# A fused embedding, interaction and MLP kernel on one core: the second contraction and the MLP of a chunk moved into one step, layer 0 a slice earlier, one transpose replaced by a DMA

## What is computed

```python
e = stack([tbl_f[ids[:, f]] for f in range(39)], axis=1)      # [1024, 39, 16]
X0 = e; Xi = X0; res = []
for W, b in ((W0, b0), (W1, b1), (W2, b2)):                    # 128 outputs each
    Wr = W.reshape(128, 39, Xi.shape[1])
    Xi = einsum('hjk,bjd,bkd->bhd', Wr, X0, Xi) + b[None, :, None]
    res.append(Xi.sum(axis=2))
h = concatenate(res + [dense_ctx], axis=1)                     # [1024, 400]
h = maximum(h @ W_top1 + b_top1, 0.0)                          # 512
h = maximum(h @ W_top2 + b_top2, 0.0)                          # 256
y = h @ W_top3                                                 # [1024, 1]
```

## Time and profile before

| | us |
|---|---|
| median of 3 runs | 1438.17 (1437.16 to 1438.38) |
| the profiled execution, its time | 1436.21 |
| its span, first to last instruction | 1434.4 |
| PE busy | 1313.6 (92%) |
| DVE busy | 1082.4 (75%) |
| ACT busy | 1066.5 (74%) |
| POOL busy | 892.8 (62%) |
| mean granted PE clock | 0.972 of 2.4 GHz |

### The profile page before, as it was taken

One profiled execution on the slowest core, in us unless ns is written; L12 is line 12 of the kernel. 1 busy time (PEld: TensorE's weight loads), 2 busy tenths in 40 slices (PEclk: granted clock), 3 DMA queues, 4 the chain that ended last, 5 costly groups with the idle time before them and its releaser, 6 DMA issues.

```text
span 1434.4 us, 23609 instructions
## 1 busy us (share of the span) xinstructions
PE 1313.6 (92%) x6157; PEld 1061.7 (74%) x6157; DVE 1082.4 (75%) x2678; ACT 1066.5 (74%) x3372; POOL 892.8 (62%) x663
## 2 busy tenths in 40 slices
PE   3179999999999999999999999999999999999986
PEld 3158777777788777887778777887778878887765
DVE  3068989898867987688766988679876988679930
ACT  2238888789867887688867888678876899678942
...
DMA packets 53451, 87.27 MB, mean 61 GB/s; under 512 B 15136, under 2 KB 37152, under 8 KB 52032
## 3 DMA queue, kind: packets, MB, share of 16 engines
...
q10 hardware_dynamic: 156, 0.48, 0.1%
...
## 4 chain that ended last, share of the span: by engine, by line
PE 54%; POOL 19%; issue 12%; DVE 8%; DMA 3%; ACT 2%; SPq 1%; ACTq 0%; POOLq 0%; DVEq 0%
PE ring L927 12%; PE ring L929 11%; PE ring L928 11%; POOL pairs L396 6%; POOL pairs_lo L407 6%; PE side L825 5%; POOL e_in L364 5%; PE l_ps L812 3%; DVE terms L754 3%; POOL blocks L418 3%; PE side L851 3%; PE l_ps L814 3%; PE l_ps L813 2%; DVE x_s L709 2%; DMA x_rep<-x_t 2%
## 5 line engine op out<-in xcount | busy, mean ns | idle before, releaser
L597 ACT ACTIVATE terms<-ring,e_both 128x128 f32<-128x128 f32 x2944 | 832.2, 399 | 242.9 <-PE ring L929 237.4
L754 DVE SCALAR_TENSOR_TENSOR terms<-ring,e_both,terms 128x128 f32<-128x128 f32 x1792 | 508.4, 344 | 96.7 <-PE ring L929 93.6
L927 PE MATMUL ring<-w_hi,x_hi 128*128 128x512 f32 (+1 forms) x1280 | 546.4, 427 | 32.5 <-DVE terms L754 25.2
L929 PE MATMUL ring<-w_hi,x_lo 128*128 128x512 f32 (+1 forms) x1280 | 500.4, 391 | 0.0
L928 PE MATMUL ring<-w_lo,x_hi 128*128 128x512 f32 (+1 forms) x1280 | 498.8, 390 | 0.0
L709 DVE TENSOR_REDUCE x_s<-terms 128x32 f32<-128x800 f32 x512 | 489.0, 976 | 0.2
L364 POOL DMA_INDIRECT e_in<-in_tbl,idx x312 | 305.8, 980 | 88.6 <-issue 79.0
L407 POOL TENSOR_TENSOR pairs_lo<-pairs,pairs_hi 117x1024 fp32r<-117x1024 f32 (+1 forms) x104 | 250.0, 2404 | 168.0 <-ACT pairs_hi L497 167.0
L927 PEld LDWEIGHTS ring<-w_hi,x_hi 128*128 128x128 f32 x1280 | 242.9, 190 | 106.8 <-DVE terms L754 38.5
L396 POOL TENSOR_TENSOR pairs<-x_rep,pairs 117x1024 f32<-117x1024 f32 (+1 forms) x104 | 250.4, 2408 | 93.2 <-DMA pairs<-x_t 93.2
L928 PEld LDWEIGHTS ring<-w_lo,x_hi 128*128 128x128 f32 x1280 | 243.6, 190 | 49.1
...
## 6 DMA issues: line engine op xcount, KB each, us to landing
pairs<-x_t SPq DMA_DIRECT2D x312, 156.0 KB
...
e_in<-in_tbl,idx POOLq DMA_INDIRECT x312
...
```

The lines of the kernel that those rows point to most:

```text
L597: last = nc.scalar.activation(term(d, ACT_BEFORE[d][g] + i), twos(ring[:, (GROUPS * d + g) % RING, i * H:(i + 1) * H]), ACT.Copy, scale=e_ ...
L754: nc.vector.scalar_tensor_tensor(out=acc, in0=y, scalar=e_of[:, j, d:d + 1], in1=acc, op0=ALU.mult, op1=ALU.add).then_inc(dve_unit, 1)
L927: nc.tensor.matmul(acc, x1_hi[:, x], w1_hi[:, w], start=True, stop=False)
L929: nc.tensor.matmul(acc, x1_lo[:, x], w1_hi[:, w], start=False, stop=True).then_inc(y_group, 1)
```

## The change

1. The table of places: layer 0's tiles 0 to 6 are made a slice earlier (7 to 13), tile 7 stays in slice 15; a tile is multiplied at groups 4 and 6; x1 of the first half leaves at (14, 7) and (14, 9), z0 at (15, 7).
2. x0t goes from slices 6, 7 to 5, 6, with the copies of the gathered rows (`COPY_SLICE`, `MOVE_SLICE`) a slice earlier, and the gathers are spread anew.
3. G of chunk c-1 is done in step c at groups 2, 5, 8 of slices 2, 3, 4, 7, 8 and at (9, 1); its blocks are made a slice ahead, with 4 slots in place of 3.
4. The MLP of chunk c-1 follows in the same step, slices 9 to 14. Step 9 is gone.
5. `xb` comes no longer from PE: `e_cur` is stored with d outermost, written to DRAM (`x0_write`, 128 x 16 x 39, after pair tile 11 on SP) and read back (`xb_back`, at the head of the next step).
6. G's columns are kept in groups: the evacuation (`evacuate_g`) reads and writes runs of 8, where before it wrote every 16th word; z0, dense and h2 are reordered to match; a block has its samples innermost.
7. `dense_t` has 128 rows, 112 of them zero, so that all of h1's matmuls have 128 rows.
8. SP's program is written out instead of looped.

```diff
-    Z2_SLICES, Z2_FROM, Z2_AT_ONCE = (0, 1, 2), 4, 2
-    XB_SLICES, XB_AT = (0, 1), 6
-    DENSE_SLICE = 2
-    H1_SLICE, H1_AT = 3, (6, 7, 8, 9)
-    H2_SLICE = 4
-    Y_SLICE, Y_AT = 5, 7
-    COPY_SLICE, CUR_FROM, MOVE_SLICE = 2, 4, 5
-    X0T_SLICES = (6, 7)
-    G_FIRST = 8
+    Z2_SLICES, Z2_FROM, Z2_AT_ONCE = (9, 10, 11), 4, 2
+    DENSE_SLICE = 11
+    H1_SLICE, H1_AT = 12, (6, 7, 8, 9)
+    H2_SLICE = 13
+    Y_SLICE, Y_AT = 14, 7
+    COPY_SLICE, CUR_FROM, MOVE_SLICE = 1, 3, 4
+    X0T_SLICES = (5, 6)
+    G_AT = [(d, g) for d in (2, 3, 4, 7, 8) for g in (2, 5, 8)] + [(9, 1)]
+    G_OUT_AT = [(d, g + 3) if g < 7 else (d + 1, 1) for d, g in G_AT]
...
-    L0_AT = [(1, 2) if d == D - 1 else (3, 5) for d in range(D)]
-
-    X1_HI_AT = {1: (6, 7), 0: (15, 4)}
-    X1_LO_AT = {1: (7, 1), 0: (15, 6)}
-    Z0_AT = {1: (7, 7), 0: (15, 8)}
+    L0_AT = (4, 6)
+
+    X1_HI_AT = {1: (6, 7), 0: (14, 7)}
+    X1_LO_AT = {1: (6, 9), 0: (14, 9)}
+    Z0_AT = {1: (7, 7), 0: (15, 7)}
...
-    BLOCK_FIRST, BLOCK_SLOTS = 7, 3
-
-    GATHERS = (3, 3, 3, 3, 3, 0, 6, 5, 1, 1, 2, 2, 1, 2, 1, 3)
-    INDEX_SLICE = 6
+    BLOCK_SLOTS = 4
+
+    GATHERS = (3, 2, 2, 2, 0, 5, 5, 1, 2, 2, 2, 2, 2, 2, 4, 3)
+    INDEX_SLICE = 5
...
+                def x0_write():
+
+                    after(sp, e_cur_ready, c + 1)
+                    after(sp, xb_in, 16 * c)
+                    sp.dma_start(x0_dram.rearrange("d b f -> b d f"), e_cur).then_inc(x0_out, 16)
+
+                def xb_back():
+
+                    after(sp, x0_out, 16 * c)
+                    after(sp, block_made, G_GROUPS * (c - 1))
+                    sp.dma_start(xb[:, :, :], x0_dram.rearrange("d (b g) f -> (d b) g f", g=G_GROUPS)
+                                 ).then_inc(xb_in, 16)
...
-                        nc.scalar.activation(e_cur[:, :, :], e_mid[:, 0:FIELDS, :], ACT.Copy).then_inc(e_cur_ready, 1)
+                        after(act, x0_out, 16 * c)
+                        nc.scalar.activation(e_cur, e_mid[:, 0:FIELDS, :].rearrange("p f d -> p d f"),
+                                             ACT.Copy).then_inc(e_cur_ready, 1)
...
                     nc.scalar.activation(
-                        g_t[:, :, g::G_GROUPS],
-                        side[:, g % 2, 0:SAMPLES_PER_G * GCOLS].rearrange("p (b j) -> p j b", j=GCOLS),
+                        g_t[:, :, g * SAMPLES_PER_G:(g + 1) * SAMPLES_PER_G],
+                        side[:, g % 2, 0:SAMPLES_PER_G * GCOLS].rearrange("p (j b) -> p j b", j=GCOLS),
                         ACT.Copy).then_inc(g_ready, 1)
```

More of the change, by code:

```diff
@@ L159, in build_tower @@
         x2_r = sb("x2_r", [P, G_GROUPS, H])
-        xb = [sb(f"xb{i}", [P, G_GROUPS, FIELDS]) for i in range(2)]
-        blocks = sb("blocks", [P, BLOCK_SLOTS, SAMPLES_PER_G, GCOLS])
+        xb = sb("xb", [P, G_GROUPS, FIELDS])
+        blocks = sb("blocks", [P, BLOCK_SLOTS, GCOLS, SAMPLES_PER_G])
         g_t = sb("g_t", [P, GCOLS, P])
@@ L230, in build_tower, with by_group, scale_of @@
         block = ctx.enter_context(nc.Block())
+        def by_group(ap):
+            return ap.rearrange("p (g b) -> p b g", b=SAMPLES_PER_G)
+        def scale_of(j, d):
+            return e_mid[:, j, d:d + 1] if d < CUR_FROM else e_cur[:, d, j:j + 1]
         def twos(ap):
@@ L350, in step @@
                         x2_write(c, q)
-            steps(sp, step)
+            steps(sp, step, unrolled=True)
             for c0, c1 in ((0, CHUNKS - 1), (CHUNKS - 1, CHUNKS)):
@@ L377, in _, with step @@
                 gather(0, f)
-            def step(c, odd, layer1, following, previous, mlp, gathers):
+            def step(c, odd, layer1, following, previous, earlier, gathers):
                 def next_index():
@@ L426, in step @@
                         multiply_pairs(*made)
-                    if previous and BLOCK_FIRST <= d < BLOCK_FIRST + G_GROUPS // 2:
-                        for i in range(2):
-                            make_block(2 * (d - BLOCK_FIRST) + i)
                     if layer1 and following and d < INDEX_SLICE:
@@ L437, in step @@
                             gather(c + 2, f)
+                    if previous:
+                        for n in range(G_GROUPS):
+                            if G_AT[n][0] == d + 1:
+                                make_block(n)
                     if made:
@@ L560, in step @@
                         side_work(d)
-                        if previous and G_FIRST <= d:
-                            evacuate_g(c - 1, 2 * (d - G_FIRST))
+                        if previous:
+                            for n in range(G_GROUPS):
+                                if G_OUT_AT[n][0] == d:
+                                    evacuate_g(c - 1, n)
                         if following and d == X0T_SLICES[0] + 1:
@@ L893, in side_work @@
                             after(pe, x2_in, 16 * c)
+                        if r == G_BEFORE_X0T and following:
+                            after(pe, x0t_ready, 4 * (c + 2))
                         n = G_GROUPS * (c - 1) + r
```

216 lines of the change are left out of this document (102 added, 114 removed).

## The result

| | before | after |
|---|---|---|
| median, us | 1438.28 (1437.16 to 1438.90, 4 runs) | 1418.23 (1414.05 to 1420.63, 4 runs) |
| the profiled execution, its time | 1436.21 | 1419.39 |
| its span | 1434.4 | 1417.6 |

The ratio is 0.9858, 95% interval 0.9833 to 0.9884: 20 us faster. The forecast was 1414, with a range of 1394 to 1437. The two profiled spans differ by 16.8 us, and it is this difference that is taken apart here; the forecast's sum for it was 24.7.

What follows compares the result with a forecast made beforehand. PE bounds the kernel (busy 92%). xb -19.2, h1 -10.4, a seventh MLP beside layer 1 +15.1, tail -6.7, waits -5 and +1.5 make -24.7: 1436.2 to 1411.5, as a median 1414 us; range 1394 to 1437.

Steps and rivals of the forecast that it cites:

- likeliest case: Whole kernel: the forecast's own case, 1404 to 1424 us, chance 0.48.
- Tail: Behind layer 1's end: -7.7 as only x2's return holds the G's, -2 slots and evacuation, +3 clock; -6.7 us.
- the dearer case of the prediction: Tail: by the skill's rule alone all of it to y could run at half rate, the sum 6 us worse.
- xb: Slices 0 and 1: by DMA, PE saves 2 x 1.2 us in each of 8 steps, -19.2; the DMAs cost nothing.
- Rivals C and D: x2's read too late for (2, 2), 1449 at 5 us late; or PE waits for returned xb; together 0.10.
- h1: MLP's h1 quarters: 128 rows throughout saves 0.33 us a quarter, 1.3 a chunk, -10.4 (0 to -11.5).
- POOL and ACT in slices 2 to 4: New waits: POOL at 9.5 us in slices 1 to 3, ACT about 10 in 3, 4, 7; 2 us a step.
- rival B: Load only changes place: POOL, ACT, light edge slices set pace, waits 10 us a step, h1 nothing; about 1431, 0.20.
- The step's edge: Slices 14, 15, 0, 1: DVE has 35.1 us against PE's 31.9, so 3.2 us of waiting, no gain.
- Slices 7 and 8: PE has G's there now (6.8 + 1.6 and 8.2 + 1.6), and its 1.8 us wait for DVE shrinks to about 0.5.
- G's evacuation: On ACT: about 0.5 us each with runs of 8, where 752 ns before; 4 us of ACT per step, off the path.
- Rival A: Tables fit better: edge, POOL and ACT waits nearly vanish (3 us a step), full steps under 157; about 1397, chance 0.22.

Runs made afterwards that it cites:

- run 2: Changed kernel with the 16 xb transposes put back on PE at (0, 6) and (1, 6), xb still coming by DMA: 1474.13 us.
- run 3: Changed kernel with h1's fourth matmul of each quarter back to 16 rows: 1477.43 us.
- run 11: Changed kernel with the first half's x1 and z0 back in slice 15, at groups 4, 6 and 8: 1465.32 us.
- run 9: Changed kernel again, 1456.59 us; with z0's addition at (10, 4), G's (7, 2) at (5, 1) and x0t's last evacuation at (7, 1), 1431.60 us.
- Runs 4 to 6: Changed kernel with, in turn, G's (7, 2) moved to (5, 1); z0's addition moved to (10, 4); both: 1468.32, 1454.86, 1437.05 us.
- run 10: Changed kernel with G's evacuation written to every sixteenth word again: 1455.92 us.

## Why the prediction was right, and where it was not

The time lies in the likeliest case (1404 to 1424), 4 us above the number. The sum was 24.7 us and the spans differ by 16.8. By place, between the two traces of the first chip: +0.5 before step 0, -3.2 in step 0, +0.5 in steps 1 to 6 together, -4.1 in step 7, -10.5 behind it. Steps 1 to 6 were forecast at 6 x 161 = 966 us, 10.5 under the 976.5 of the kernel before, and took 977.0: they gave nothing. The rest was forecast to give 14.2 and gave 17.3. So the terms of the removed work were about right and the tail gave more than forecast, while the waits of a full step were put too low, and that the number came out within 4 us is in part luck. By parts, from the same two traces where no run is named:

- **Tail: -10.5, where -8.0 was expected** (-6.7, and 1.3 of the last h1). The G's begin 13.3 us after the last matmul group of layer 1, 14.1 expected. PE's wait of 13.18 us is x2's way out and back: DVE's last sums (to 1371.0), the write, and the read, issued at 1373.30 and waited for 5.2. From the first G to z2 it took 13.3 us where it had taken 13.8; -2 for slots and evacuation and +3 for the clock had been put there. The clock fell as feared, but +3 was too much: only four G's stood at the half level, in 4.1 us, and the other twelve took 0.72 each, which makes the clock's price about 1.2 us (an estimate: 4 x (1.03 - 0.72)). z2's 8.97 us are the same as before. The Trainium skill (TensorE: Matmul & The Clock Gate, "HAM oscillation") warns that idle gaps send the array back to the lower clock; the trace agrees for the first G's (0.50). That the whole tail would stay there, the dearer case of the prediction, did not come: z2's row has 1.00.
- **xb: -19.2**, 17.9 by the slices of run 2. Right, nearly. The DMAs that took its place cost nothing, and x2's read came in time for (2, 2) in every step: in step 5 it was issued at 906.96 and G began at 915.05 without a wait. Rivals C and D fall.
- **h1: -10.4**, by run 3 -12.1.
- **POOL and ACT in slices 2 to 4, 2 us a step: nothing.** Slices 2 to 4 are 9.8 us, which is all matmuls. The waits for POOL in 11, 12 and 14 went as foreseen, and slice 9's shrank to about 0.3. So POOL and ACT did not set the pace there, as rival B had it, nor was h1's term nothing. B's general point, that waits come back elsewhere, did come true, in slices 7 and 8, and the steps 1 to 6 show its size.
- **The step's edge, 3.2 us a step**: slices 14, 15, 0, 1 of step 5 take 34.9 us where 35.1 was worked out from DVE's load. Right, and run 11 shows how little its place matters.
- **Slices 7 and 8: the step that failed.** The prediction said "DVE's 1.8 shrinks to about 0.5" and so put the two at 18.7 us. They took 24.0 in the mean of steps 1 to 6, 32 us more over the six. Elsewhere a full step was 3.4 us under the forecast. The two partly cancel, by luck: that, more than the terms, is why 161 was near the mean of 162.8. Three things were wrong:
  - G at (7, 2) needs PSUM that x0t still holds, and ACT frees it at group 3; the sharing is named in the section on the kernel before, and the table alone shows that (7, 2) comes ahead of group 3 on ACT, but it was not followed through. This wait is 2.3 us a step.
  - DVE's addition of z0's halves was priced at 0.35 from a row where POOL made no products.
  - The 1.8 did not shrink to 0.5: beside the G's of slices 7 and 8 PE still waits for DVE's sum, 1.6 us in the mean of the six steps, 1.43 to 1.52 in four of them, and 1.39 with the addition out of the way (run 9).

  The clock's share in slice 7 is 1.6 us each time it falls (12.67 against 11.09), three times in six steps. Run 9 shows the first two causes together: without them the same two slices are 20.3 us (with one G fewer in them, 0.54), on a chip where the changed kernel has 25.9. With that G counted it is 20.8, still 2.1 over the 18.7, and 0.9 of this is DVE's wait. Runs 4 to 6 show that the two causes depend on each other.
- **G's evacuation**: 0.5 forecast, 0.469 measured, and its worth is about 4 us by the pieces of run 10, 1.8 of them in the tail; inside the steps it is nearly off the path, as forecast. The copy to `e_cur` went from 743 to 1360 ns, as put, and slice 1 still is 8.20 us, so it is hidden. The Trainium skill (SBUF — State Buffer, "Door 1: The DMA port swizzle") says that SBUF has lines of 16 bytes and that an access which goes on to a new line pays for it. The trace agrees in sign: runs of 8 words made the evacuation faster (run 10 goes back in the write alone, 761 ns), reading every 16th word made the copy slower.
- **Rival A** said the tables fit better, with waits of 3 us a step and full steps under 157. The waits at the edge stayed, and full steps were 160.7 to 166.8; even with all three edits of run 9 the mean is 160.7.

Left open: why the clock falls behind some waits of 2.2 to 2.4 us and not behind others, and what makes slice 6 longer on the later chips (by 0.4 to 1.2 us) and puts a wait for ACT's terms into slice 7 there. How much of the spread of the changed kernel (1414 to 1420.6) comes from the two stalls was not measured.
